# First chunk's up-products formed for all eight experts ahead of the routing, chosen by index from on-chip copies

## The reference, cut to what matters

```
# x is (1, 2048, 128); E = 8 experts, hidden F = 256, TOP_K = 2
logits = mean(x, axis=1) @ Wr + br          # one row of 8 logits for the whole sequence
routing = softmax(logits); routing = softmax(routing * scale(capacity))
top_w, top_i = top_k(routing, 2); top_w = softmax(top_w)
h = gelu(x @ W1[e] + b1[e]);  y = h @ W2[e] + b2[e]
out = layer_norm(sum over the two chosen e of top_w * y + x)
```

## Time and profile before

| what | us |
|---|---|
| median of 3 runs (876.28 to 877.75) | 877.64 |
| the profiled execution's own time | 879.34 |
| its span | 877.6 |
| TensorE busy | 718.9 (82%) |
| VectorE busy | 665.1 (76%) |
| ScalarE busy | 484.5 (55%) |
| mean granted TensorE clock | 0.911 |

### The profile page before, as it was taken

One profiled execution on the slowest core, in us unless ns is written; L12 is line 12 of the kernel. 1 busy time (PEld: TensorE's weight loads), 2 busy tenths in 40 slices (PEclk: granted clock), 3 DMA queues, 4 the chain that ended last, 5 costly groups with the idle time before them and its releaser, 6 DMA issues.

```text
span 877.6 us, 15527 instructions
## 1 busy us (share of the span) xinstructions
PE 718.9 (82%) x5089; PEld 530.0 (60%) x5091; DVE 665.1 (76%) x2281; ACT 484.5 (55%) x723; POOL 277.1 (32%) x584
## 2 busy tenths in 40 slices
PE   4999999768999566799999989678778797886294
PEld 2455555427999543477777678465345675786263
DVE  6758677733444377889983499999899999999757
ACT  4877686304555326456555276467696775822153
POOL 3410421336666305400000034051432576770000
PEclk9999999787999869799999999797998997988788
DMA  8764000075887400000000000000000001101001
GB/s 152 118 98 77 26 17 10 26 172 154 230 229 236 160 1 1 0 2 1 1 1 2 1 1 2 1 2 1 0 1 1 1 2 47 51 1 33 0 1 48
DMA packets 47367, 41.94 MB, mean 48 GB/s; under 512 B 7376, under 2 KB 44112, under 8 KB 47280
## 3 DMA queue, kind: packets, MB, share of 16 engines
q1 hardware_dynamic: 29488, 19.95, 8.2%
q0 software_dynamic: 11456, 14.62, 8.0%
q10 hardware_dynamic: 6336, 6.32, 3.0%
HBM read 39.69 MB, written 9.57 MB: 56 GB/s over the span
## 4 chain that ended last, share of the span: by engine, by line
DVE 34%; PE 20%; issue 4%; ACT 4%; POOLq 1%; DVEq 1%; POOL 0%; ACTq 0%
DVE big L1595 6%; PE bank L2138 5%; PE bank L2042 5%; DVE cand L1513 4%; PE bank L2121 4%; DVE rm L1353 3%; DVE hacc L1508 3%; DVE big L1584 2%; DVE cand L1359 2%; DVE cand L1534 2%; PE bank L2315 2%; DVE big L1581 2%; DVE top L1529 2%; ACT big L1868 1%; PE bank L2327 1%
## 5 line engine op out<-in xcount | busy, mean ns | idle before, releaser
L2121 PE MATMUL bank<-ident,big 128*128 128x128 f32 x512 | 82.6, 311 | 31.3 <-DVEq L1618 21.9
L1868 ACT ACTIVATE big<-bank 128x512 f32<-128x512 f32 x128 | 71.0, 597 | 52.5 <-PE bank L2121 51.7
L2121 PEld LDWEIGHTS bank<-ident,big 128*128 128x128 f32 x512 | 63.3, 157 | 59.1 <-DVEq L1618 22.9
L2042 PE MATMUL bank<-kk,qq 64*128 64x512 f32 x256 | 78.8, 734 | 19.8 <-ACT big L1838 19.2
L1838 ACT ACTIVATE big<-bank,negm 128x2048 f32<-128x2048 f32 x32 | 62.7, 1958 | 47.1 <-DVE fsc L1645 36.8
L2049 PEld LDWEIGHTS bank<-parts,adjT 128*128 128x128 bf16 x1536 | 86.6, 98 | 3.0 <-issue 2.1
L2049 PE MATMUL bank<-parts,adjT 128*128 128x128 bf16 x1536 | 87.9, 219 | 0.6 <-DVE xn L1438 0.6
L1595 DVE SCALAR_TENSOR_TENSOR big<-big,st 128x2048 f32<-128x2048 f32 x32 | 75.2, 2388 | 5.2 <-PE bank L2121 5.2
L399 POOL DMA_INDIRECT ys_scratch<-big,parts x62 | 60.0, 967 | 33.2 <-ACT big L754 23.4
L844 PE MATMUL bank<-big,xn 128*128 128x512 f32 x128 | 62.2, 608 | 5.7 <-DVE big L546 5.7
L828 PE MATMUL bank<-xnT 128*128 128x512 f32 x128 | 62.0, 609 | 2.3 <-DVE xnT L535 2.3
(11 more groups left out here) (380 smaller groups left out, 1517.4 us busy)
## 6 DMA issues: line engine op xcount, KB each, us to landing
big<-in_L_ffn_w_dram SPq DMA_DIRECT2D x93, 128.0 KB
big<-in_adj_dram POOLq DMA_DIRECT2D x8, 512.0 KB, 7.3
big<-xs_scratch ACTq DMA_DIRECT2D x31, 132.0 KB
kk<-in_adj_dram POOLq DMA_DIRECT2D x4, 512.0 KB, 8.1
qq<-in_adj_dram POOLq DMA_DIRECT2D x4, 512.0 KB, 10.0
xs_scratch<-hacc SPq DMA_DIRECT2D x9, 132.0 KB
xs_scratch<-hacc ACTq DMA_DIRECT2D x8, 132.0 KB
res<-in_x_dram SPq DMA_DIRECT2D x4, 256.0 KB, 6.3
```

The costliest lines, as they stand in the source:

```text
L1868: nc.scalar.activation(MT[:, 4 * q:4 * q + 4, s * P:(s + 1) * P], bank[:, 5 + q % 2, :].rearrange("p (j i) -> p j i", j=4), ACT.Copy).then ...
L2042: nc.tensor.matmul(bank[:, c, :], qq[lo:lo + DA, (g * G + s) * P:(g * G + s + 1) * P], kk[lo:lo + DA, c * CH:(c + 1) * CH], start=True, st ...
L2121: mm = nc.tensor.transpose(bank[:, 5 + q % 2, j * P:(j + 1) * P], mk[:, s, jt * P:(jt + 1) * P], ident[:, :])
```

## The change: what it does

Sixteen products `up_first(k)` (8 experts by 2 halves) of the first 512 rows with each expert's first weights are formed on TensorE before the routing is known, alternating between banks 0 and 1. ScalarE copies each with `take_first(k)` to `spec`, which lies in `adjT`, no longer used by then. Six of them stand behind `turn_h(1)` and ahead of `flag_sum` of group 7 on TensorE (on ScalarE behind `take_h(1)` and ahead of `copy_MT` of group 7), ten behind `turn_h(3)` and ahead of `turn_h(4)` (on ScalarE between `take_h(3)` and `take_h(4)`). `up(0)` is gone; TensorE's order at the end is up(1), y(0), up(2), y(1), up(3), y(2), y(3). ScalarE loads the two indices into registers of its own and its first four Gelus read `spec` by them. A Gelu of one column stands ahead of that on ScalarE, right after the last Exp of the routing. VectorE waits on a semaphore of its own for the index.

```
+        NS1 = ED * HCD
+        AHEAD1 = 6
+        spec = adjT[...] as fp32 [P, e, u, n]
...
+                def take_first(k):
+                    act.wait_ge(s1_done, k + 1)
+                    nc.scalar.activation(spec[:, k // HCD, k % HCD, :], bank[:, k % 2, :], ACT.Copy).then_inc(s1_out, 1)
...
                     if g == NG - 1:
                         take_h(0)
                         take_h(1)
+                        for k in range(AHEAD1):
+                            take_first(k)
...
-                for i in range(2, len(XS)):
+                for i in range(2, len(XS) - 1):
                     take_h(i)
+                for k in range(AHEAD1, NS1):
+                    take_first(k)
+                take_h(len(XS) - 1)
...
                 nc.scalar.activation(one[7], one[6], ACT.Exp).then_inc(d_ex, 1)
+                nc.scalar.activation(gelu_in[:, :], ones[:, 0:1], ACT.Gelu)
+                act.wait_ge(d_idx, 1)
+                chosen = [bass.ds(act.value_load(idx8[0:1, k:k + 1], ...), 1) for k in range(2)]
...
                 act.wait_ge(d_w1, 4)
                 for c in range(NC):
                     for u in range(2 * HCD):
-                        v = c * 2 * HCD + u
-                        act.wait_ge(d_h, v + 1)
+                        v = (c - 1) * 2 * HCD + u
+                        if c:
+                            act.wait_ge(d_h, v + 1)
+                            src = bank[:, v % 4, :]
+                        else:
+                            src = spec[:, chosen[u // HCD], u % HCD, :]
-                        nc.scalar.activation(hid[:, c % 2, u, :], bank[:, v % 4, :], ACT.Gelu,
+                        nc.scalar.activation(hid[:, c % 2, u, :], src, ACT.Gelu,
...
+                def up_first(k):
+                    e, u = divmod(k, HCD)
+                    if k < 2:
+                        pe.wait_ge(d_xT_out, k + 1)
+                        pe.wait_ge(d_ldw, 32)
+                    else:
+                        pe.wait_ge(s1_out, k - 1)
+                    nc.tensor.matmul(bank[:, k % 2, :], w1all[:, e, u * P:(u + 1) * P], xnT[:, 0:CH], start=True,
+                                     stop=True).then_inc(s1_done, 1)
...
                         turn_h(0)
                         turn_h(1)
+                        for k in range(AHEAD1):
+                            up_first(k)
...
-                for i in range(2, len(XS)):
+                for i in range(2, len(XS) - 1):
                     turn_h(i)
+                for k in range(AHEAD1, NS1):
+                    up_first(k)
+                turn_h(len(XS) - 1)
+                pe.wait_ge(s1_out, NS1)
...
                 pe.wait_ge(d_w1, 4)
-                up(0)
+                up(1)
                 pe.wait_ge(d_w2, 2)
                 for c in range(NC):
-                    if c + 1 < NC:
+                    if c and c + 1 < NC:
                         up(c + 1)
```

More of the change, by code:

```diff
@@ L1119, in build @@
         (d_ld, d_ldw, d_xn, d_xT, d_xT_out, d_meanb, d_nm, d_ex, d_w1, d_w2, d_h, d_hid, d_y,
-         d_out, d_store, d_stat, d_res, d_xn_p, d_nmr, d_yn) = names(
+         d_out, d_store, d_stat, d_res, d_xn_p, d_nmr, d_yn, d_idx, s1_done,
+         s1_out) = names(
              "d", "ld", "ldw", "xn", "xT", "xT_out", "meanb", "nm", "ex", "w1", "w2", "h", "hid", "y", "out", "store",
-             "stat", "res", "xn_p", "nmr", "yn")
+             "stat", "res", "xn_p", "nmr", "yn", "idx", "s1_done", "s1_out")
         FIRST_TILES = (NG - 1) * G
         EARLY = 2 * TPC
+        NS1 = ED * HCD
+        AHEAD1 = 6
+        spec = adjT[:, :, :].rearrange("p a b -> p (a b)").bitcast(F32)[:, 0:NS1 * CH].rearrange(
+            "p (e u n) -> p e u n", e=ED, u=HCD)
+        gelu_in = sb("gelu_in", [P, 1])
         XS = [(0, 4), (4, 8), (8, 12), (12, FIRST_TILES), (FIRST_TILES, NT)]
@@ L1753, in _ @@
                 ch.link(nc.vector.max(r8[:, M8, :], r8[:, EX8, :]))
-                v = op(nc.vector.max_index(idx8[:, :], r8[:, M8, :], r8[:, EX8, :]))
+                nc.vector.max_index(idx8[:, :], r8[:, M8, :], r8[:, EX8, :]).then_inc(d_idx, 1)
                 nc.vector.tensor_tensor(one[6], r8[:, M8, 1:2], r8[:, M8, 0:1], ALU.subtract).then_inc(d_nm, 1)
-                since(v)
+                dve.wait_ge(d_idx, 1)
                 dve.wait_ge(d_ldw, 32)
@@ L1987, in _ @@
                 nc.scalar.activation(one[7], one[6], ACT.Exp).then_inc(d_ex, 1)
+                nc.scalar.activation(gelu_in[:, :], ones[:, 0:1], ACT.Gelu)
+                act.wait_ge(d_idx, 1)
+                chosen = [bass.ds(act.value_load(idx8[0:1, k:k + 1], min_val=0, max_val=ED - 1), 1) for k in range(2)]
                 def norm(c):
@@ L1996, in _ @@
                     for u in range(2 * HCD):
-                        v = c * 2 * HCD + u
-                        act.wait_ge(d_h, v + 1)
+                        v = (c - 1) * 2 * HCD + u
[3 more added lines that the diff above has]
+                        else:
+                            src = spec[:, chosen[u // HCD], u % HCD, :].rearrange("p a n -> p (a n)")
                         if u == 0 and c >= 2:
                             act.wait_ge(d_y, c - 1)
-                        nc.scalar.activation(hid[:, c % 2, u, :], bank[:, v % 4, :], ACT.Gelu,
+                        nc.scalar.activation(hid[:, c % 2, u, :], src, ACT.Gelu,
                                              bias=db1[:, u // HCD, u % HCD:u % HCD + 1]).then_inc(d_hid, 1)
@@ L2311, in up @@
                     for u in range(2 * HCD):
-                        v = c * 2 * HCD + u
+                        v = (c - 1) * 2 * HCD + u
                         if v >= 4:
-                            pe.wait_ge(d_hid, v - 3)
+                            pe.wait_ge(d_hid, 2 * HCD + v - 3)
                         nc.tensor.matmul(bank[:, v % 4, :], dw1[:, u // HCD, (u % HCD) * P:(u % HCD + 1) * P],
```

## The result

The changed kernel takes 873.56 us (median of 8 runs, 871.7 to 874.7) against 877.38 us of the kernel before (8 runs, 875.74 to 880.12): a ratio of 0.9958, 95% interval 0.9947 to 0.997, or 3.8 us less. The forecast was 873.5 us and -4.14 us.

The account below looks back on a forecast made before the run. A chain of waits on TensorE from 834.64 us to y(2), then on VectorE, bounds the kernel. -3.44 + 0 + 0.3 - 0.55 + 0 - 0.45 = -4.14 us takes the 877.64 median to 873.5; own range 872.7 to 874.6.

Parts of the forecast that it names:

- both covers: TensorE's idle stretches ahead of group 7's flags and turn_h(4): six products fit for +0.3 us, ten for 0.
- A: Tail on TensorE: up(0) leaves, up(1) pays the cold start, y(0) starts earlier by eight warm records: -3.44 us.
- B: Chunk 0's Gelus on ScalarE, with index loads and table load, end 1.7 us before y(0) can start: 0.
- C: Six products ahead of group 7's flags delay the flag matmul, so VectorE waits: about +0.3 us.
- D: Group 7 on a warm clock: turn_mk and pv end earlier, gain capped by VectorE's own work: -0.55 us.
- E: Ten products between turn_h(3) and turn_h(4) nearly fill TensorE's idle stretch but fit: 0, bounds 0 and +0.6 us.
- F: After turn_h(4)'s wait: warm transposes -0.25 and warm product with Wr -0.2, together -0.45 us.
- the clock stayed up across the routing: Rival: clock stays high through the routing, up(1) costs 3.44 us, another -1.7, total 871.8 us; 8%.
- ScalarE was late: Rival: chunk 0's Gelus cost 3 us more, y(0) starts at 841.4, gain shrinks by 1.3, total 874.8 us; 6%.
- the rival on the slower side: Rival: clock falls while products alternate between two banks, ten at 1.71 us each, total 881.9 us; 3%.

Follow-up runs that it names:

- warm: The changed kernel plus six unread 128x512 fp32 matmuls on TensorE behind the product with Wr; ratio to the kernel before 0.9936, flags to end 71.4 us.
- banks4_warm: The changed kernel with products over four banks and six unread matmuls behind the product with Wr; ratio to the kernel before 0.9933, flags to end 71.2 us.
- best: banks4_warm once more, beside the changed kernel on one chip; ratio to the kernel before 0.9947, flags to end 71.6 us.
- banks4: The changed kernel with its products rotating over four banks instead of two; ratio to the kernel before 0.9954, flags to end 73.3 us.
- banks4_warm_table: banks4_warm without the one-column Gelu, so the table load stays in its old place; ratio to the kernel before 0.9924, flags to end 71.75 us.
- after_again: The changed kernel unedited, profiled once more on another chip; ratio to the kernel before 0.9956, flags to end 74.0 us.
- unused: The changed kernel with products formed and copied but unread, up(0) back in the tail; ratio to the kernel before 0.9988, flags to end 77.4 us.
- before_warm3: The kernel before plus unread matmuls: five ahead of group 7's flags, nine ahead of turn_h(4), six across the routing; ratio 0.9972, flags to end 75.1 us.

## Why the prediction was right, step by step

The mechanism came out as forecast: the tail lost one block, its successor paid the cold start, and both covers held. That the measured median meets the forecast to 0.1 us is partly luck. The forecast started from a median of three runs of before (877.64), 0.3 us above that of all eight (877.38), and the gain was 0.3 us smaller than forecast (3.8 for 4.14).

- **A (tail, -3.44).** y(0) starts 5.73 us after the first record of up(1), 5.43 forecast: the cold part was as long as before plus 0.3. So the step brought 3.14 us in this pair of profiles. Cold blocks of sixteen records took 8.87 and 9.47, cold blocks of eight 5.48 to 6.54; the difference of the smallest two is 3.39. The term stands; a few tenths either way are the clock's. One part of its working is misread: the 0.28 us that four records at 0.86 and four at 0.43 leave of 5.43 is not rounding. With the clock at 1.00 a first block of eight took 3.70 us where TensorE had paused ahead of it (warm, banks4_warm) and 3.43 where it had not (best). It changes nothing in the sum, since up(1) inherits it. The reading of the clock is a little off too: in the kernel before the 807 stretch has 0.78, so the clock came back about 4.7 us after 802.73 and not within 4.5. That the gain is 3.44 and not the 5.43 that up(0) took was the step that mattered.
- **B (Gelus, 0).** Right, with more room than I had: the index loads ran on the sequencer under the table load (my lower bound), the Gelu of 512 columns from SBUF took 0.64 us, and they ended at 834.62, 3.1 us ahead of y(0), not 1.7.
- **C (late flags, +0.3).** From first flag write to VectorE's read it is 1.35 us after (799.65 - 798.30) and 0.91 before (801.33 - 800.42, rows of before in the earlier trace rows and the chain): +0.44. Mis-sized by 0.1. The 0.35 us in brackets is that wait.
- **D (warm group 7, -0.55).** VectorE's last add_pv stands 15.91 us after the first flag write, 16.12 before: net of C -0.2, forecast -0.25. The cap held: TensorE's pv of group 7 began 3.1 us earlier in the profile, of which 2.1 came from further up, and VectorE did not wait for it.
- **E (ten products, 0).** The products ended at 823.67 and tile 15 was ready at 823.75: the cover was used to the last tenth. The last copy (823.70 to 824.29) stood ahead of take_h(4), which is why the chain runs over TensorE and ScalarE there; it costs at most 0.1 us (banks4, where turn_h(4) waits for VectorE, has 17.70 us from the last add_pv to up(1), and this kernel 17.76).
- **F (warm transposes and product, -0.45).** From the last add_pv to up(1) it is 17.76 us, 18.10 before: -0.34. The transposes took 0.49 for 0.66, the product with Wr 0.36 for 0.57.

The terms of one pair of profiles add to 3.14 + 0.2 + 0.34 = 3.7 us, as they must, since they cut one stretch into pieces, and the medians differ by 3.8; terms of a few tenths (C, D, F) rest on that one pair; the rest of the 5.8 us between the spans (2.1) is there at the flags already, ahead of the change. Of the rivals, the clock stayed up across the routing in none of the eight profiles in which TensorE had nothing to do there (every first up block is cold in them), and ScalarE was late only in banks4_warm_table, where it was meant to be. The products between two banks kept their warm pace in every profile, 0.91 to 0.94 us each, so the rival on the slower side did not come about in them. The argument against it was weaker than it looked, though. It was that the clock rose to 1.00 during the transposes of turn_mk, which alternate between two banks too; in three profiles the clock fell during just these transposes (last section).

## What to carry to other kernels

Work that depends on a late choice can be done for every choice beforehand, if the engines are idle then; its price is not its own time but what stands behind it in the engine's order, so count the idle stretch in single instructions, as here with six and ten, and try the splits on both sides: here two products too many in either cover cost 1.2 to 1.7 us. Work that is taken off the front of a chain that begins cold is worth its warm time only (here 3.1 to 3.4 us and not 5.43), since the next in line pays the cold start.

## What was not expected of the hardware

The granted clock can fall when TensorE has been idle for much less than the 4 to 5 us read before. In the changed kernel's second profile it had worked to 810.8 with one pause of 0.34 us since the attention's products, waited 1.45 us, and was at the transposes again when the clock fell; the same stretches:

```profile
810.00:811.00 1.00, 0.81 (x4) 1.00 0.11 29
811.00:812.00 1.00, 0.00 (x0) 1.00 0.85 307
812.00:813.00 1.00, 0.74 (x7) 1.00 0.93 217
813.00:814.00 1.00, 0.75 (x8) 1.00 0.72 103
814.00:815.00 1.00, 1.00 (x7) 0.51 1.03 33
817.00:818.00 1.00, 1.00 (x8) 0.78 0.00 0
```

It did so in 3 of the 11 profiles with TensorE kept busy up to there (after_again, unused, before_warm3), and during the filling matmuls in 2 of 5 (best, before_warm3). In both places TensorE had been busy only in part for 2 to 3 us just before. The other eight and three profiles look much the same there and kept 1.00, so that alone does not tell them apart. What sets it off was not tried and stays open. It cost little in group 7 (0.2 us to the last add_pv), because VectorE is the cap there, and 0.7 us in best.
